# Token lists of a mixture of experts: from scatters in memory to products of one-hots on TensorE

## What is computed

```python
x = x + _L0_attn_ref(_layernorm(x), ...)      # mixer, then MLP with 704 hidden values
x = x + _L0_ffn_ref(_layernorm(x), ...)       # experts
# _L0_ffn_ref, E = 8, TOP_K = 2, M = 896:
router_probs = jax.nn.softmax(x_flat @ gate_w, axis=-1)
topk_w, topk_idx = jax.lax.top_k(router_probs, TOP_K)
topk_w = topk_w / jnp.sum(topk_w, axis=-1, keepdims=True)
sort_idx = jnp.argsort(topk_idx.reshape(-1))
x_rep_sort = jnp.take(x_flat, sort_idx // TOP_K, axis=0)
h = jax.lax.ragged_dot(x_rep_sort, w1, group_sizes)
h = jax.nn.silu(h) * jax.lax.ragged_dot(x_rep_sort, w3, group_sizes)
out_sort = jax.lax.ragged_dot(h, w2, group_sizes)      # then weighted by topk_w and summed
```

## Time and profile before

| | us |
|---|---|
| median of 3 runs | 785.66 (784.55 to 786.02) |
| profiled execution | 792.77 |
| its span in the trace | 790.9 |
| busy PE, DVE, ACT, POOL | 708.4, 594.6, 235.5, 286.2 |
| first projection of tile 0 starts | 409.04 |

### The profile page before, as it was taken

How to read it: one execution, slowest core, us unless ns; L and a number is a source line. 1 busy time by engine, 2 the same in 40 slices (tenths; PEclk the granted TensorE clock), 3 DMA queues, 4 the chain that set the end, 5 groups by cost and what they waited for, 6 DMA issues and landing times.

```text
span 790.9 us, 10048 instructions
## 1 busy us (share of the span) xinstructions
PE 708.4 (90%) x2695; PEld 453.8 (57%) x2696; DVE 594.6 (75%) x1457; ACT 235.5 (30%) x480; POOL 286.2 (36%) x475
## 2 busy tenths in 40 slices
PE   6979889999998999987039999999999999999992
PEld 4445655586466657646015666666666666666661
DVE  4889999689738875536407888888888888888870
ACT  1556655744755444321011111111111111111110
POOL 3023533323223432542521444333344433334422
PEclk9999999999999999999559999999999999999997
DMA  9302003000310080581068711111111211111111
GB/s 326 132 1 107 1 1 108 0 1 28 89 46 1 27 305 1 66 128 54 1 233 277 250 28 32 33 27 27 27 27 27 33 33 27 27 27 27 27 19 15
DMA packets 32669, 52.26 MB, mean 66 GB/s; under 512 B 4419, under 2 KB 24323, under 8 KB 32624
## 3 DMA queue, kind: packets, MB, share of 16 engines
q1 hardware_dynamic: 24096, 41.60, 17.1%
q0 software_dynamic: 8544, 10.30, 8.0%
HBM read 42.23 MB, written 9.81 MB: 66 GB/s over the span
## 4 chain that ended last, share of the span: by engine, by line
PE 68%; DVE 15%; issue 6%; POOL 4%; DMA 4%; ACT 2%; DVEq 0%; POOLq 0%; SPq 0%
PE ps L995 28%; PE ps L1008 14%; PE ps L697 4%; PE ps L685 4%; PE ps L711 4%; PE ps L406 3%; DVE big L1496 3%; DVE big L1516 2%; PE ps L585 2%; PE ps L461 2%; DVE big L1972 2%; POOL lists L2087 1%; PE ps L528 1%; PE ps L475 1%; DMA lists<-big 1%
## 5 line engine op out<-in xcount | busy, mean ns | idle before, releaser
L1972 DVE STREAM_TRANSPOSE big<-big 32x224 f32<-32x224 f32 x608 | 244.8, 403 | 9.1
L995 PE MATMUL ps<-big 128*128 x624 | 243.5, 544 | 1.1 <-ACT big L1403 1.1
L995 PEld LDWEIGHTS ps<-big 128*128 128x128 f32 x624 | 119.4, 192 | 106.5 <-issue 104.6
L1008 PE MATMUL ps<-big 128*128 x546 | 124.5, 380 | 2.2 <-DVE big L1992 1.4
L2015 POOL TENSOR_TENSOR big<-big 128x1 f32<-128x1 f32 x153 | 48.8, 319 | 203.9 <-DVE big L1980 153.9
L1008 PEld LDWEIGHTS ps<-big 128*128 128x128 f32 x546 | 100.8, 190 | 15.1 <-issue 3.0
L1409 ACT ACTIVATE big<-ps 128x896 f32<-128x896 f32 x39 | 35.8, 917 | 218.0 <-PE ps L995 218.0
L406 PE MATMUL ps<-big 128*128 128x128 f32 (+1 forms) x327 | 55.5, 285 | 35.7 <-DMA big<-lists,big 23.3
L406 PEld LDWEIGHTS ps<-big 128*128 128x128 f32 (+1 forms) x327 | 42.4, 149 | 67.7 <-issue 32.3
L1987 DVE TENSOR_TENSOR big<-big,ps 128x896 f32<-128x896 f32 x39 | 42.4, 1088 | 48.6 <-PE ps L995 48.5
L2241 POOL DMA_INDIRECT out_rows<-big x39 | 62.9, 1614 | 23.2 <-issue 23.2
(11 more groups left out here) (175 smaller groups left out, 911.4 us busy)
## 6 DMA issues: line engine op xcount, KB each, us to landing
big<-in_w SPq DMA_DIRECT2D x24, 896.0 KB, 11.0
big<-cum_rows SPq DMA_DIRECT2D x16, 512.0 KB, 5.4
out_rows<-big SPq DMA_DIRECT2D x4, 512.0 KB
xn_rows<-big SPq DMA_DIRECT2D x4, 512.0 KB
big<-in_hidden SPq DMA_DIRECT2D x1, 1536.0 KB, 11.6
big<-in_in_proj SPq DMA_DIRECT2D x1, 1288.0 KB, 6.6
big<-in_gate SPq DMA_DIRECT2D x1, 640.0 KB, 12.6
big<-in_up SPq DMA_DIRECT2D x1, 640.0 KB, 8.7
```

The source lines that it names most:

```text
L995: last = mm(bank(bk + n)[:, 0:HALF], xT[:, k, :], expert_cols(e, off + k * M + n * HALF, HALF), start=(k == 0), stop=(k == KD - 1))
L1008: last = mm(bank(7)[:, 0:D], hTs[:, half, j * P:(j + 1) * P], expert_cols(e, 2 * KD * M + j * D, D), start=(j == 0), stop=(j == MB - 1))
L1972: last = V.transpose(hTs[c * SQ:(c + 1) * SQ, half, :].rearrange("p (j t) -> p j t", j=MB)[:, :, q * SQ:(q + 1) * SQ], ha[q * SQ:(q + 1) * ...
```

## The change

Nothing is scattered to memory any more. A token's slot in its expert's list is split into a list number (which block of 128 entries) and a place within it. `route_hot` (VectorE) works both out: `is_q` marks the block, `place` is the remainder. `route_list` (VectorE) multiplies the chosen expert's one-hot with `is_q` into `hot_list`, a one-hot over 8 x 16 lists. `slots` (GpSimd) takes the scatters' position: per block and choice it compares `place` with 0 to 127 and multiplies by the token number and by the weight, four operations a block, 64 in all. `place_` (TensorE) multiplies `hot_list` by that, 2 products a block, summed in PSUM over all tokens: the result holds all lists. `lists_copy` (ScalarE) takes it out, and `choose` (TensorE) picks the 39 tiles' lists with `chosen`, a one-hot from the table (`table`, VectorE). Token numbers are stored less 2048, and place and 2048 are added at the end, so that empty entries point to dummy rows.

With the lists go the input `empty`, its copy, the read-back and the gather of the table. SyncE loads experts 3 to 7 once the first two gathers have landed. Five products keep TensorE busy before tile 0. `zero` and the new buffers lie in columns that mixer and later experts use. The steps of the mixer stand in another order on all engines.

```diff
@@ SyncE
-            sp.wait_ge(rec_out, 16 * CH * TOP * SEQS)
-            sp.dma_start(rec0, lists[0:P, :]).then_inc(rec0_in, 16)
-            for e in range(EARLY + 1, SOON):
-                load_next(e)
-
             for half in range(2):
                 sp.wait_ge(xg_in[half], 16)
-            for e in range(SOON, E):
+            for e in range(EARLY + 1, E):
                 load_next(e)
@@ TensorE
+            def place_(n, t):
+                pe.wait_ge(hot_placed, nth(n, CH, t))
+                pe.wait_ge(hot_ready, TOP * (n + 1 if n < SEQS - 1 or t < CH // 2 else n + 2))
...
+                for k in range(TOP):
+                    last = mm(bank(STATES)[:, 0:2 * P], hot_list[n][:, t, k, :], hot_slot[n][:, t, k, :],
+                              start=(n + t + k == 0), stop=(n == SEQS - 1 and t == CH - 1 and k == TOP - 1))
...
+            def choose():
+                pe.wait_ge(lists_taken, 1)
+                pe.wait_ge(chosen_ready, 1)
+                pe.wait_ge(pos_taken, SEQS + 1)
+                for i in range(2):
+                    last = mm(bank(MISC)[:, i * TILES:(i + 1) * TILES], lists[:, i * P:(i + 1) * P], chosen, start=True, stop=True)
+                last.then_inc(recT_ps, 1)
...
             half_logits(0)
+            place_(0, 0)
+            place_(0, 1)
+            place_(0, 2)
+            place_(0, 3)
             turn_half(1)
             half_logits(1)
+            place_(1, 0)
...
             positions(3, HALVES[0][1])
+            place_(2, 0)
...
             positions(4, HALVES[1][1])
-
-            pe.wait_ge(recg_in, 16)
-            for i in range(2):
-                last = transposed(bank(7)[:, i * TILES:(i + 1) * TILES],
-                                  recg[0:TILES, :].rearrange("t (s two) -> t two s", two=2)[:, i, :], TILES)
-            last.then_inc(recT_ps, 1)
-
-
+            place_(3, 0)
...
+            choose()
...
+            keep_warm(DIAG, WARM_ROWS)
@@ VectorE
+            def route_hot(n, ts=ALL, seq=None):
...
+                hot_.then(V.tensor_tensor(upto_q[:, q, :], pos.unsqueeze(2).to_broadcast([P, m * TOP, LIST]), firsts, ALU.is_ge))
+                hot_.then(V.tensor_reduce(q1[:, q], upto_q[:, q, :], AX, ALU.add))
+                hot_.then(V.tensor_scalar(q0[:, q], q1[:, q], float(P), -float(P), ALU.mult, ALU.add))
+                hot_.then(V.tensor_tensor(to, pos, q0[:, q], ALU.subtract))
...
+                hot_.then(V.tensor_tensor(is_q[seq][:, q, :], q0[:, q].unsqueeze(2).to_broadcast([P, m * TOP, LIST]), firsts, ALU.is_equal))
...
+            def route_list(n, k, ts=ALL, seq=None):
...
+                V.tensor_tensor(hot_list[seq][:, ts, k, :].rearrange("p t (e i) -> p t e i", e=E),
...
             add_mlp(3, 0)
+            route_hot(0)
             add_mlp(3, 1)
             ln2_stats(3, HALVES[0][1], 2)
+            route_list(0, 0, ALL, None)
             xn_(3, HALVES[0][1], 3)
+            route_list(0, 1, ALL, None)
+            route_hot(1)
+            route_list(1, 0, ALL, None)
             add_mlp(3, 2)
-            route_slots(2)
+            route_list(1, 1, ALL, None)
             add_mlp(3, 3)
@@ GpSimd
-            def scatter(n, t, seq):
-                g.wait_ge(lists_in, 16)
-                g.wait_ge(rec_ready, n + 1)
+            def slots(n, t, seq):
+                g.wait_ge(o_taken, SEQS * CH)
+                g.wait_ge(ssy_ready, SEQS * CH)
+                g.wait_ge(place_ready, n + 1)
                 for k in range(TOP):
-                    G.indirect_dma_start(lists, bass.IndirectOffsetOnAxis(ap=slot[seq][:, t, k:k + 1], axis=0),
-                                         rec[seq][:, t, k, :], None).then_inc(rec_out, 16)
+                    for i in range(2):
+                        last = G.tensor_scalar(hot_slot[seq][:, t, k, i * P:(i + 1) * P], cst[:, C_SLOT:C_SLOT + P],
+                                               place[seq][:, t, k:k + 1], rec[seq][:, t, k, i:i + 1], ALU.is_equal, ALU.mult)
+                last.then_inc(hot_placed, 1)
```

More of the change, by code:

```diff
@@ L191, in build @@
         late_end = at[0]
+        at[0] = (EARLY + 1) * EXPERT
+        hot_list = tuple(cols(CH, TOP, E * LIST) for _ in range(SEQS))
+        hot_slot = tuple(cols(CH, TOP, 2 * P) for _ in range(SEQS))
+        lists = cols(2 * P)
+        upto_q = cols(CH * TOP, LIST)
+        is_q = tuple(cols(CH * TOP, LIST) for _ in range(SEQS))
+        ge_row = cols(TILES, E - 1)
+        gn_row = cols(TILES, E - 1)
+        assert at[0] <= SOON * EXPERT
         at[0] = E * EXPERT
@@ L724, in _ @@
             dt_(0)
+            z_(0, 0)
             xbc_(0, 0)
@@ L956, in _ @@
             mlp_up(3, 4)
+            positions(2)
             mlp_gate(3, 5)
@@ L960, in _ @@
             mlp_down(3, 2)
-            positions(2)
             turn_half(0)
@@ L1810, in _ @@
+            ln2_stats(0)
+            conv_taps(3, 1)
+            y_(2, 0)
+            h1_(1, 3)
+            conv_taps(3, 2)
+            h2(1)
+            off(2, 1)
+            conv_taps(3, 3)
+            conv_taps(3, 4)
+            conv_taps(3, 5)
+            h2T1(1)
+            state(2, 1)
             scores(2, 2)
             scores(2, 3)
-            y_(2, 0)
-            h1_(1, 3)
-            ln2_stats(0)
-            state(2, 0)
-            conv_taps(3, 0)
-            h2(1)
@@ L1929, in _ @@
             xn_(4, HALVES[1][1], 3)
+            route_hot(2)
             route_pick(3, HALVES[0][1], 3, half_rt)
@@ L2223, in _, with gather @@
             g.wait_ge(pads_out, 32)
-            def gather(i, odd, first=False):
+            def gather(i, odd):
                 at_half = gidx[:, odd:odd + 1]
-                G.tensor_copy(at_half, rec0[:, 0:1] if first else ids[:, bass.ds(i, 1)]).then_inc(gidx_ready, 1)
+                G.tensor_copy(at_half, ids[:, bass.ds(i, 1)]).then_inc(gidx_ready, 1)
                 g.wait_ge(gidx_ready, i + 1)
```

766 lines of the change are left out of this document (405 added, 361 removed).

## The result

The changed kernel takes **795.43 us** (793.13 to 798.29), beside 785.84 (784.55 to 786.64) for the kernel before in the same session: a ratio of 1.0119, interval 1.0096 to 1.0143. The forecast was 776.9, 1.1% faster. The time lies outside its range (769 to 787), slower instead of faster.

What follows compares the result with a forecast made beforehand. Between mixer and expert tiles a DMA-only chain (scatter landing, list read-back, gather) was taken as the bound. First tile 3.4 us earlier, 5.8 with the clock, plus 3.0 for the stall: 8.8 off 785.66 gives 776.9 us, range 769 to 787.

Steps and rivals of the forecast that it cites:

- GpSimd's comparison: Price of each of 64 one-hot comparisons on GpSimd: 0.33 us, with ends 0.19 and 0.61.
- the last normalization: VectorE's last normalization at the mixer's end, waiting for GpSimd's second `ln2_scale` behind 20 comparisons: 2.3 us later.
- GpSimd becomes the bound: Rival: comparisons at 0.61 us delay the last normalization and VectorE before tile 0; 790.5 us, chance 0.10.
- The port: After the last normalization, 44 comparisons delay VectorE's two-input operations through the shared SBUF port: 3.6 us, ends 0 and 13.
- VectorE's chain: VectorE's work from the last normalization to the end of the table: 23.0 us, where it was 20.9 before.
- `positions` behind the products: TensorE's products stand ahead of both `positions`; at half clock 8 could hold VectorE 1 to 2 us, at full clock nothing.
- After the table: From the table's end to tile 0: products and copies 1.7, gather 3.0, transposes and copy 1.35, sum 6.05 us.
- The clock: Tile 0's first projections on TensorE: products and five warming ones win back 2.4 of 2.7 us lost to the lower clock.
- The stall at 340 us: TensorE's waits beside scatters and expert 2's weight load: 3.0 us won back without scatters, ends 0 and 4.2.
- The mixer's order: Reshuffled mixer steps on nearly every engine: taken as 0, ends +4 and -4 us.
- The loads: Expert weight loads moved to start with the tiles: costed at nothing, since they have slack before the tiles needing them.
- handover: Stretch between the mixer's end and the first expert tile: tile 0 was to start 3.4 us earlier.

Runs made afterwards that it cites:

- price run: Changed kernel with a row of single operations added at its end, on GpSimd and then VectorE, all other engines idle: 820.82 us, one execution.
- the two experiments: Kernel before with only the mixer's new order: 781.62 us; changed kernel with the mixer's old order: 800.02 us.
- before's second profile: Kernel before, nothing edited, profiled once more: one execution of 787.64 us, with a profile span of 785.8 us.

## Why the prediction was wrong, point by point

- **The failed step: GpSimd's comparison, "I take 0.33", ends 0.19 and 0.61.** It is 0.79. The working ran from `TENSOR_TENSOR` rows and then argued that one input instead of two should be cheaper. The price run shows that the form with scalars is the dearer one: 0.522 with one immediate, 0.782 with two pointers, 0.442 for two tensors. So even the upper end was no bound; the nearest row was of another instruction. The Trainium skill, "GPSIMD Engine Reference", section 3.1, gives 1.03 cycles an element for the smallest elementwise bodies, which at its 1.2 GHz is an estimated 0.86 ns a column; measured here are 3.34 ns a column and 0.35 us fixed, and the measurement decides.
- **What hung on it.** The 20 comparisons took 16.8 us of the gap, not 6.6, and the last normalization slipped by 11.6 us, not 2.3. The remaining 44 ended at 408.2 us. The rival "GpSimd becomes the bound" named this place and this mechanism and a threshold of 0.5 us; it got 0.10, though no row of a two-pointer form spoke for less. Its 790.5 was worked out at 0.61.
- **The port, 3.6 us.** Half as large, and with another side that the prediction didn't have. Beside comparisons VectorE's two-input operations over 16 columns take 235 (L1667), 200 (L1705) and 187 ns (L1666), means of 4; with GpSimd idle, in the run with all on VectorE, 176, 177 and 176. Over VectorE's chain it is 1.8 us (worked out below). Those over 512 columns are not slowed (684 ns against 686), but some of the comparisons beside them are; all that comparisons lost beside VectorE's work is 3.4 us, on GpSimd, which was the bound. The earlier trace rows was a row of `TENSOR_TENSOR` on GpSimd. The rule of the Trainium skill, "SBUF — State Buffer", section "SBUF: two separate sides", gives the pair of ports to whichever engine's operation starts first, for the whole instruction. The trace agrees at 176.64 and not here: the L1740 of 378.78 begins 0.40 us into a comparison and takes its usual 0.68, while the comparison takes 1.68. VectorE was held by GpSimd all the same, for 10.3 us, but through TensorE's queue.
- **`positions` behind the products.** The prediction saw this ("8 of them could hold VectorE for 1 to 2 us") and priced it by TensorE's clock. It cost 4.48 and 5.83 us, because the products themselves waited for comparisons.
- **VectorE's chain, 23.0 us.** The size comes out, in part by luck: 372.68 to 405.94 is 33.3 us, less the two waits of 10.3 is 22.95, but this has the delay beside comparisons in it, which was to come on top. In the run with all on VectorE the same steps take 370.43 to 399.79, 29.36 us, less 8.19 for the 32 comparisons among them: 21.17. So the chain by itself was put 1.8 us too high, and the port delays it by 1.8.
- **After the table, 6.05.** 1.1 us too small: from the first product of `choose` (410.81) to tile 0 (417.98) are 7.2 us, 2.5 until the gather starts at 413.32 (1.7 forecast) and 4.7 behind it (4.35). There `keep_warm`'s 4.61 us hide the gather, which landed in 3.03 in the run without them. Ahead of it stand 2.6 us that the sum hadn't (408.20 to 410.81), since the last products wait for GpSimd's last comparison and not for the table.
- **The clock, 2.4.** Right: 2.76 in the table above. The run without warming shows where 1.7 of it comes from.
- **The stall at 340 us, 3.0.** Wrong: it belonged to one execution. The prediction took a difference within a profile 7 us above the median and used it against the median, and should have asked what in that profile made up the 7.
- **The mixer's order, 0 (4 either way).** It wins 3 to 6 us by the two experiments. TensorE's idle time, which the prediction looked for at 80 to 120 us, went at 240 to 280.
- **The loads, at nothing.** Right for the tiles: both kernels take 9.26 us a tile from the third on, and no tile waits. The gain of an undisturbed gather was in the 6.05; moving the loads back costs 5.2 us of handover, and moving them later in the kernel with scatters shortens it by 3.6.
- **Not foreseen:** 1.5 us less from the last tile's epilogue to the end: 20.8 to 21.2 us in the profiles of kernels without lists in memory, 22.4 to 22.7 with them. It lies behind the issue of the last addition (12.1 us from there to the end in before's second profile, 10.6 after). No experiment asked for its cause, and it stays open.

The errors in sum, against the second profile of before: handover +18.0 where -3.4 was forecast; mixer -3.75 where -3.0 was, by another cause; first tile -2.8 where -2.4 was; the end -1.5.

## What to carry to other kernels

Price an operation by a row of the same instruction with the same kinds of operands; where there is none, its upper bound is open, and the rival that hangs on it deserves a real share. Before work is put on an engine, look at what already stands in that engine's queue behind it: 20 comparisons ahead of a 0.7 us operation cost 11.6 us, and with 28 of the same 64 put into 32 us of idle time, and masks and `positions` moved up with them, a loss of 1.2% became a gain of 1.6%. A profile whose time is far from the median has something in it that the median has not: find it before it becomes a term of the sum.

## What the runs showed of the hardware

- On GpSimd `TENSOR_SCALAR` with two per-partition pointers takes 0.35 us and 3.34 ns a column (0.461 at 32, 0.782 at 128, 2.063 at 512); pointers cost more than immediates (0.782 against 0.632), and `TENSOR_TENSOR` (0.442) and `COPY` (0.284) over 128 columns cost less. The same operation on VectorE comes every 0.26 us.
- Back-to-back comparisons of this form on GpSimd held back VectorE's two-input operations over 16 columns a little (235, 200 and 187 ns against 176, 177 and 176) and those over 512 columns not at all (684 against 686). The other way a comparison beside such a 512-column operation took up to 1.68 us instead of 0.79.
- The landing of the last scatter took 10.5 to 10.7 us in every profile with scatters but the first (10.63, 10.71, 10.52; 9.48 there), with the DMA engines otherwise idle.
- The same gather of 128 rows took 2.8 to 3.1 us alone and 5.9 to 6.7 beside weight loads.
